# New orders for the first and last batches of a decoder layer, three more PSUM banks for the last one, and products of the identity where TensorE waits

## What is computed

```python
def ffn(x, gamma_x, gamma_slot, slot_embeds, w1, w2):
    xn = rms_norm(x, gamma_x)
    se = rms_norm(slot_embeds, gamma_slot)
    logits = jnp.einsum('bsd,etd->bset', xn, se)
    dispatch = jax.nn.softmax(logits, axis=1)
    slots = jnp.einsum('bsd,bset->betd', xn, dispatch)
    h = jax.nn.gelu(slots @ w1, approximate=False)
    processed = h @ w2
    combine = jax.nn.softmax(logits.reshape(b, s, e * t), axis=-1)
    return jnp.einsum('bnd,bsn->bsd', processed.reshape(b, e * t, d), combine)

x = x + attn(layernorm(x), Wq, bq, Wk, bk, Wv, bv, Wo, bo)
x = x + xattn(layernorm(x), ctx, ctx, mask, Wq2, ...)
x = x + ffn(layernorm(x), gamma_x, gamma_slot, slot_embeds, w1, w2)
```

## Time and profile before

| | us |
|---|---|
| median of 3 runs | 2020.74 |
| lowest and highest | 2017.63, 2021.1 |
| the profiled execution | 2018.85 |
| its span, first to last instruction | 2017.0 |
| PE busy (matmul) | 1812.1 (90%) |
| VectorE, ScalarE, POOL busy | 1081.9, 961.5, 418.7 |
| mean granted clock of TensorE | 0.947 |
| self attention of batch 0, 1, 2 added up (L1005) at | 105.6, 220.8, 334.0 |

### The profile page before, as it was taken

One profiled execution on the slowest core, in us unless ns is written; L12 is line 12 of the kernel. 1 busy time (PEld: TensorE's weight loads), 2 busy tenths in 40 slices (PEclk: granted clock), 3 DMA queues, 4 the chain that ended last, 5 costly groups with the idle time before them and its releaser, 6 DMA issues.

```text
span 2017.0 us, 41529 instructions
## 1 busy us (share of the span) xinstructions
PE 1812.1 (90%) x16912; PEld 1596.0 (79%) x16912; DVE 1081.9 (54%) x2224; ACT 961.5 (48%) x1688; POOL 418.7 (21%) x349
## 2 busy tenths in 40 slices
PE   2566799999999999999999999999999999998876
PEld 1343688889888888888888888888888888888866
DVE  4333456556565555556565656556565656554422
ACT  2211354555555464555545464555545464555442
POOL 1000111222212221222221222122221222122222
PEclk7565799999999999999999999999999999999889
DMA  4000000000000000000000000000000000000000
GB/s 142 1 8 1 8 1 7 9 7 9 1 15 1 15 1 9 7 7 9 2 14 1 15 1 10 7 7 9 2 14 1 15 2 9 7 1 6 1 6 6
DMA packets 20851, 19.88 MB, mean 10 GB/s; under 512 B 9921, under 2 KB 19777, under 8 KB 20289
## 3 DMA queue, kind: packets, MB, share of 16 engines
q1 hardware_dynamic: 20672, 17.06, 2.9%
HBM read 12.86 MB, written 4.19 MB: 8 GB/s over the span
## 4 chain that ended last, share of the span: by engine, by line
PE 81%; DVE 9%; issue 4%; ACT 3%; SPq 1%; POOL 1%; DMA 0%; POOLq 0%; DVEq 0%; ACTq 0%
PE ps L347 19%; PE ps L348 17%; PE ps L349 17%; PE ps L432 4%; PE ps L469 3%; PE ps L563 2%; PE ps L609 2%; PE ps L647 2%; PE ps L579 1%; PE ps L452 1%; PE ps L544 1%; PE ps L499 1%; PE ps L638 1%; PE ps L389 1%; DVE sl_lo L900 1%
## 5 line engine op out<-in xcount | busy, mean ns | idle before, releaser
L1238 POOL TENSOR_TENSOR h_lo<-h_f,h_hi 128x512 fp32r<-128x512 f32 x256 | 330.4, 1291 | 1186.0 <-DVE h_hi L1110 1186.0
L347 PE MATMUL ps<-w_hi,h_hi 128*128 128x256 f32 x1024 | 304.9, 298 | 32.7 <-issue 22.2
L347 PE MATMUL ps<-sl_hi,w_hi 128*128 128x256 f32 x1024 | 304.2, 297 | 22.0 <-DVE cb_lo L900 21.6
L348 PE MATMUL ps<-w_hi,h_lo 128*128 128x256 f32 x1024 | 292.1, 285 | 0.0
L349 PE MATMUL ps<-w_lo,h_hi 128*128 128x256 f32 x1024 | 292.0, 285 | 0.0
L348 PE MATMUL ps<-sl_hi,w_lo 128*128 128x256 f32 x1024 | 290.8, 284 | 0.0
L349 PE MATMUL ps<-sl_lo,w_hi 128*128 128x256 f32 x1024 | 290.7, 284 | 0.0
L1110 DVE CAST h_hi<-h_f 128x512 fp32r<-128x512 f32 x256 | 132.2, 516 | 241.0 <-ACT h_f L860 240.9
L347 PEld LDWEIGHTS ps<-w_hi,h_hi 128*128 128x128 f32 x1024 | 198.2, 194 | 62.5 <-issue 51.1
L977 DVE TENSOR_REDUCE mx<-ps 128x8 f32<-128x2048 f32 x64 | 146.4, 2288 | 151.9 <-PE ps L432 151.9
L860 ACT ACTIVATE h_f<-ps 128x512 f32<-128x512 f32 x256 | 152.4, 596 | 156.5 <-PE ps L349 156.0
(11 more groups left out here) (193 smaller groups left out, 4141.5 us busy)
## 6 DMA issues: line engine op xcount, KB each, us to landing
x<-in_x SPq DMA_DIRECT2D x16, 256.0 KB, 2.7
out<-acc SPq DMA_DIRECT2D x16, 256.0 KB, 2.2
g_w<-in_w SPq DMA_DIRECT2D x2, 1024.0 KB, 6.1
cx<-in_ctxT SPq DMA_DIRECT2D x16, 77.0 KB, 2.0
g_wqk<-in_wqk SPq DMA_DIRECT2D x1, 1024.0 KB, 6.9
g_se<-in_se SPq DMA_DIRECT2D x1, 1024.0 KB, 9.6
biases<-in_bias SPq DMA_DIRECT2D x1, 640.0 KB, 4.9
mk_i<-in_mask SPq DMA_DIRECT2D x16, 38.5 KB
```

Source lines behind the costliest of these rows:

```text
L347: te.matmul(o, lhs[0], rhs[0], start=first, stop=False)
L348: te.matmul(o, lhs[1], rhs[0], start=False, stop=False)
L1238: Q_.tensor_tensor(h_lo[:, part, :], h_f[:, part, :], h_hi[:, part, :].bitcast(f32), ALU.subtract)\
```

## The change

It has five parts.

1. `START` and `FINISH` take the place of `FIRST`, `LAST` and the partial passes: lists with the batch written at each step (c0, d0, m0 for batch 0, m-1 for the last), for each engine, with turns of the banks of their own. Before the loop they cover c, d and m of batch 0, c and d of 1 and c of 2. The loop's list is untouched.
2. `idle`: TensorE multiplies the identity by itself into bank 7, 276 times in all, at 51 places, 270 of them before oproj of batch 1.
3. The preparation of weights and slots is rewritten and spread: gamma goes into the split of w1 and of the slots, the squares go to ScalarE with its accumulator, the scaling of the slots (2048 elements a partition) and w2's lower part to POOL. The columns of the biases are made after batch 0's statistics.
4. SP's order of loads: wq2, slots, gammas, w1, w2 and wkv2 go before the context, wo and wo2.
5. In the last batch `hidden` has banks 1 to 4, `comb` bank 0, and its tiles lie in xa instead of beside those of `dispatch`.

```diff
+START = dict(
+    pe="""
+        s0.idle.10 c0.xt.1 s0.idle.14 c0.q c0.k c0.v c0.scores.0 s0.idle.8 c0.mt.0 s0.idle.4 c0.shifted.0 s0.idle.6
...
+FINISH = dict(
+    pe="""
...
+        m-1.hidden.0.1 l-2.combine.3 m-1.dispatch.1 m-1.hidden.0.2 m-1.hidden.0.3 m-1.lt.2 m-1.slots.1 m-1.outer.0.0
...
+MISC_START = """
+    c0.xt1 c0.mt.0 c0.pv.0 c0.mt.1 c0.pv.1 c0.tr.0 c0.ob.0 c0.mt.2 c0.pv.2 c0.mt.3 c0.pv.3 c0.tr.1 c0.ob.1 c0.oproj
...
 def program(engine, handle, steps):
 
-    run(engine, steps, FIRST, c=0, s=0)
-    run(engine, steps, c=1, d=0)
-    run(engine, steps, c=2, d=1, m=0)
+    run_list(steps, START[engine])
     with handle.Fori(1, B - 2) as b:
         run(engine, steps, c=b + 2, d=b + 1, m=b, l=b - 1)
-    run(engine, steps, d=B - 1, m=B - 2, l=B - 3)
-    run(engine, steps, LAST, m=B - 1, l=B - 2)
+    run_list(steps, FINISH[engine])
...
+        def hidden_bank(b, q):
+
+            return 1 + q if last_batch(b) else 6 - q % 2
+
+        def comb_bank(b):
+
+            return 0 if last_batch(b) else 6
+
+        def comb_tile(b):
+
+            return (xa_hi, xa_lo) if last_batch(b) else (cb_hi, cb_lo)
...
+            def idle(_, times):
+
+                for n in range(times):
+                    te.matmul(ps[:, 7, 0:P], ident[:, :], ident[:, :], start=True, stop=True)
...
             def slots(b, c):
 
                 pe.wait_ge(s["ds_lo"], nth("ds_lo", b, c + 1))
-                if c:
+                if c and last_batch(b):
+                    pe.wait_ge(s["sl_lo"], nth("sl_lo", b, c))
+                elif c:
                     pe.wait_ge(s["ge"], nth("ge", b, 4 * c))
...
+            def se_squares(_):
+
+                act.wait_ge(s["i_se"], 16)
+                for e in range(NS):
+                    last = nc.scalar.activation(se_sq[:, e, :], g_se[:, e, :], ACT.Square, accum_out=se_ss[:, e:e + 1])
+                last.then_inc(s["i_st"], 1)
...
+            def se_hi(_, dk):
+                act.wait_ge(s["i_sps"], dk + 1)
+                act.wait_ge(s["i_gxs"], 1)
+                nc.scalar.activation(W["se"][0][:, dk, :], ps[:, 5:7, :].rearrange("p u n -> p (u n)"),
+                                     ACT.Identity, scale=gxs[:, dk:dk + 1]).then_inc(s["i_shi"], 1)
...
-                dve.wait_ge(s["i_w1"], 16)
-                for dk in range(ND):
-                    last = V.tensor_scalar(stage["w1"][:, dk, :], stage["w1"][:, dk, :], gam[:, 0, dk:dk + 1], None,
-                                           ALU.mult)
-                last.then_inc(s["i_w1g"], 1)
...
+                pool.wait_ge(s["i_sr"], 4)
+                Q_.tensor_tensor(g_se[:, :, :], g_se[:, :, :], se_sc[:, :].unsqueeze(2).broadcast_to([P, NS, D]), ALU.mult)\
+                    .then_inc(s["i_xn"], 1)
+
+            def lo(_, n):
+
+                pool.wait_ge(s["i_hi"], n + 1)
+                src, (hi, low) = once(WEIGHTS[n])
+                Q_.tensor_tensor(low, src, hi.bitcast(f32), ALU.subtract).then_inc(s["i_w2lo"], 1)
...
+            load("wq2", stage["wq2"][:, :, :])
+            sp.dma_start(g_se[:, :, :], t_in["se"].rearrange("(e p) d -> p e d", p=P)).then_inc(s["i_se"], 16)
+            sp.dma_start(gam[:, :, :], t_in["gam"]).then_inc(s["i_gam"], 16)
+            load("w1", stage["w1"][:, :, :])
+            load("w2", stage["w2"][:, :, :])
+            load("wkv2", W["wkv2"][:, :, :])
             load_ctx(0)
-            load("wq2", stage["wq2"][:, :, :])
-            load("wkv2", W["wkv2"][:, :, :])
```

More of the change, by code:

```diff
@@ L145, in user_before @@
 def user_before(ring, name, batch):
+    if isinstance(batch, int):
+        rest, misc = name[1:], ring is MISC
+        for listed, shown in ((MISC_START if misc else QUAD_START, batch), (MISC_FINISH if misc else QUAD_FINISH, batch - B)):
+            token = f"{name[0]}{shown}{rest}"
+            if token in listed and token != listed[0]:
+                head, _, other = listed[listed.index(token) - 1].partition(".")
+                return RELEASE[f"{head[0]}.{other}"], int(head[1:]) % B
+            if token in listed and shown >= 0:
+                return None
+            if token in listed:
+                other = ring[-1]
+                return RELEASE[other], batch if other[0] == "c" else batch - 1
     lead = dict(c=1, d=0)
@@ L670, in hidden @@
                     pe.wait_ge(s["sl_lo"], nth("sl_lo", b, c + 1))
-                    if c or later(b):
+                    if not last_batch(b) and (c or later(b)):
                         pe.wait_ge(s["cb_lo"], nth("cb_lo", b, c))
-                if q >= 2:
+                if last_batch(b):
+                    if c:
+                        pe.wait_ge(s["ge"], nth("ge", b, n - 3))
+                elif q >= 2:
                     pe.wait_ge(s["ge"], nth("ge", b, n - 1))
@@ L713, in combine @@
                     for e in range(2):
-                        last = three(ps[:, 7, t * D:(t + 1) * D], both(CB, full, e, slice(t * P, t * P + P)),
+                        last = three(ps[:, 7, t * D:(t + 1) * D], both(comb_tile(b), full, e, slice(t * P, t * P + P)),
                                      both(PR, full, e), e == 0, e == 1)
@@ L753, in q_step @@
                 act.wait_ge(s["q_ps"], nth("q_ps", a, 1))
+                if not later(a):
+                    act.wait_ge(s["i_cols"], 1)
                 for c in range(C):
@@ L797, in ex2 @@
                 act.wait_ge(s["st2_ps"], nth("st2_ps", a, c + 1))
+                if not c and not later(a):
+                    act.wait_ge(s["i_sps"], 2)
                 if c:
@@ L1064, in xs @@
                 if not later(a):
-                    dve.wait_ge(s["i_lo"], len(WEIGHTS))
+                    dve.wait_ge(s["i_lo"], WEIGHTS.index("wq2") + 1)
                 else:
@@ L1141, in finish @@
                 last.then_inc(s["y"], 1)
-            dve.wait_ge(s["i_const"], 16)
-            V.tensor_scalar(half[:, 0:1], cols[:, NMASK:NMASK + 1], 1.0, None, ALU.add)
-            V.tensor_scalar(half[:, 1:2], cols[:, NMASK:NMASK + 1], -1.0, None, ALU.mult).then_inc(s["i_half"], 1)
-            dve.wait_ge(s["i_half"], 1)
-            dve.wait_ge(s["i_bcol"], 10 * 16)
-            for u in range(2):
-                own = slice(64 * u, 64 * u + 64)
-                last = V.tensor_copy(bcol[own, :, :], braw[own, :].rearrange("p (b c u) -> p b c u", b=3, c=C)[:, :, :, u])
@@ L1167, in lo @@
                 src, (hi, low) = once(name)
-                minus(low, src, hi).then_inc(s["i_lo"], 1)
+                if name == "w1":
+                    for dk in range(ND):
+                        last = V.scalar_tensor_tensor(low[:, dk, :], src[:, dk, :], gam[:, 0, dk:dk + 1],
+                                                      hi[:, dk, :].bitcast(f32), ALU.mult, ALU.subtract)
+                else:
+                    last = minus(low, src, hi)
+                last.then_inc(s["i_lo"], 1)
             def gammas(_):
@@ L1230, in bias @@
                 o, row, signal = ((x, bo, "x_bo"), (x1, bo2, "x1_bo"))[n - 1]
+                if not later(a):
+                    pool.wait_ge(s["i_bias"], 16)
                 pool.wait_ge(s[f"ln{n}_xh"], nth(f"ln{n}_xh", a, 1))
```

265 lines of the change are left out of this document (172 added, 93 removed).

## The result

The changed kernel takes 1885.82 us (median of 4 runs, 1885.74 to 1886.27) against 2019.18 (2016.23 to 2021.1, 4 runs) of the kernel before on the same chip: ratio 0.9341, 95% interval 0.9325 to 0.9357. Its profiled execution took 1885.74 us, with a span of 1883.9.

What follows compares the result with a forecast made beforehand. The prediction took the loop as bound by PE (1467.6 us, untouched), with waits and half clock before and behind it; gains of 74.7 (start), 4.2 (last but one) and 33.4 us (last batch) gave 1908 us, range 1893 to 1940.

## What to carry to other kernels

Before calling a loop untouched, look whether PE shows a wait without a releaser just behind the jump, and count the instructions that the change puts ahead of the loop; a few dozen idle instructions may be worth a per cent, and an experiment that adds or removes code must keep the loop's place or it measures that too. Where a chain of dependent steps leaves TensorE at half clock, idle products in the holes give the clock back, but as few as hold it: half of the number here took another 0.2% off the median. Freed banks are worth little by themselves (6 us); the order that they allow brings the rest (21 us).

## What the runs showed that I had not expected

- In this kernel TensorE stalls behind the loop's jump by 1.9 or 3.0 us a pass on the mean (3.5 at most) or not at all, and 16 instructions ahead of the loop change which: 115.2, 113.0 or 111.5 us a batch for the same body. Where it stalls, the instruction queue carries one packet of 16.4 KB more per jump (141 against 129 in 12 jumps).
- A stall of 2.78 us is followed by products at half clock (0.42 for 0.28 us), so it costs more than itself (3.7 us a pass for 3.0).
- 552 transposes in the place of 276 plain products held the clock at 1.00.
- With 84 idle products four executions of one program lie 10.6 us apart (1882.27 to 1892.88), with 276 by 0.4, with 212 by 3.0, with 148 by 1.1: with 84, whether the clock holds differs from one execution to the next.
- A fulfilled wait on PE isn't free: 352 of them at its head moved batch 0's end by 18.8 us.
- The clock brought little where the preparation had stood in the chain (6.9 us of 44.5 in batch 0) and nearly all in the batch behind it (22.2 of 24.6).
